# Nine subtractions on GpSimd, each made to wait for a point in VectorE's expert search

## The chip, the cores and the metric

The kernel runs on one core of one Trainium2 chip. The time is that of the whole execution on the device in microseconds (us), as the median of several runs. Five engines take part: TensorE (PE in the profile, its weight loads PEld), VectorE (DVE), ScalarE (ACT), GpSimd (POOL) and SyncE (SP), which issues most of the transfers. Each engine works through its own list of instructions in the order in which they were written, and waits for another engine at a semaphore.

## The reference, cut to what matters

Two layers over a batch of 4 sequences of 512 tokens, 256 wide. The part that the change concerns:

```
xn = layernorm(x)
# layer 0, attention: elu features, running sum of k*v over the sequence
kv_sum = cumsum(phi_k * v, axis=1); context = phi_q * kv_sum * SCALE; attn = context @ Wo.T + bo
# layer 0, ffn: 512 "genes" per token, the best 32 are kept
logits = (rms(xn) * norm_w) @ Wc.T / temperature
top_vals, top_idx = top_k(logits, 32)
expressed = sum(softmax(top_vals) * genes[top_idx])
ffn = tanh(expressed @ Wd.T) * xn * (expressed @ Wu.T) * scale
x = x + attn + ffn
# layer 1: a second attention with a dense swiglu (w_swiglu, w_out), and 16 experts of which
# each token takes 2, with a dense shared expert (shared_gate_up, shared_down)
```

The dense weights of layer 1 (shared_gate_up, shared_down, w_swiglu, w_out) are used as a sum of two parts of lower precision: the rounded weight h, and the low part l = w - h. The nine subtractions of the change make l.

## The kernel before, in words

A batch b is one sequence of 512 tokens. Work on batch b is held in tiles f0a to f0g (even b) and f1a to f1g (odd b), shown in the profile as fa to fg. Every engine has one list, written out by hand over all batches; a name such as `topb(0, 1)` is a call in that list, and its two numbers are the batch and the 128-token tile in it. Nothing reorders these lists.

What is done at the front (the first 110 us), with the lines of the profile:

- The expert search on VectorE, for each batch and tile: `topa` (a MAX8, L887, and a MATCH_REPLACE8, L891, both reading TensorE's result), `topb` (three more pairs on tile tk, L898 and L900), `topc` (one SCALAR_TENSOR_TENSOR with two operands in tk, L907). Each of `topb`'s six instructions raises the semaphore `tb` by one.
- `kvsum` on VectorE (L869): the running sum of a tile fb into ff. `qplus` (L873) and `context` (L878) follow from it.
- On TensorE `emturn` (transposes, L297) of what `topc` made, then `express` (the gene product), `ffn` (L313) and `oproj` (L320, L324). On ScalarE `emcopy` and `expert` between them, `eround` before `elow` (VectorE, L912), and `downt`, the tanh.
- `bolow` on VectorE (L811) makes the low part of the bias that `oproj` adds. `uptimes` (L919) multiplies the two halves of the ffn, and `joined` (L924) adds attention and ffn. `stats2`, the normalization of layer 1 and all the rest of the batch hang on `joined`.
- The preparation of the weights: SyncE loads nine pieces into stage0 to stage8 in the first microseconds, `prep(n)` on ScalarE rounds piece n into h and raises `ph` (L544), and `prep(n)` on GpSimd subtracts h from the staged piece (L1199) and raises `pl`. Pieces 0 and 1 are sgu (1024 and 384 columns), piece 2 is sdn (768), 3 to 6 are wsg, 7 and 8 wout (1024 each).
- On GpSimd the nine `prep` stand at the head of the list. Behind them come `upnorm(0)` (two instructions on fb, L1203 and L1205, which wait for the four `uptimes` of batch 0 and raise `u2`), `residual(0)` (L1210), and then the rest. `joined(0, 0)` waits for `u2`.

The first readers of the low parts are dense products of TensorE at about 110 us (`pl` at 2), and SyncE's `xback(0)`, which waits for `pl` at 9.

The lists around the change:

```
gpsimd: wduround(); prep(0); ... prep(8); upnorm(0); residual(0); qfold(0); ...
vector: ... topb(0, 0); kplus(0); topc(0, 0); topa(0, 1); vtimes(0, 0)
        topa(0, 2); ratio1(1); vtimes(0, 1); topb(0, 1); kvsum(0, 0); topc(0, 1); kvsum(0, 1); topb(0, 2); topa(0, 3); topc(0, 2); topb(0, 3)
        topa(1, 0); topc(0, 3); qplus(0); rscale(0); context(0); wdulow(); elow(0); topa(1, 1); kplus(1); uptimes(0, 0); bolow(); uptimes(0, 1)
        topb(1, 0); uptimes(0, 2); uptimes(0, 3); topb(1, 1); topa(1, 2); joined(0, 0); topc(1, 0); joined(0, 1); stats2(0); ...
```

Of the kernel before, what the change touches and what calls it, by code (L numbers as in the profile page):

```python
# [82 lines left out]
def build(nc, x, vec, cst, wqkv0, wo0, wc, genes, wdu, wqkv1, wsg, wout, gate, sgu, sdn, gu, dn, part_d, out):  # L83
    with ExitStack() as ctx:
        base = nc.sbuf_base + (-nc.sbuf_base) % 32
        ctx.enter_context(nc.sbuf_tensor("arena", [P, 53180], F32))
        s = {n: ctx.enter_context(nc.semaphore("s_" + n)) for n in SIGNALS}
# [117 lines left out]
        def ps(*key):  # L205
# [14 lines left out]
        PREP = [("sgu", sgu_h, sgu_l, sgu, 0, 1024), ("sgu", sgu_h, sgu_l, sgu, 1024, 384), ("sdn", sdn_h, sdn_l, sdn, 0, 768)] + \  # L220
            [("wsg", wsg_h, wsg_l, wsg, o, 1024) for o in range(0, 4096, 1024)] + \
            [("wout", wout_h, wout_l, wout, o, 1024) for o in range(0, 2048, 1024)]
        PREPARED = {"sgu": 2, "sdn": 3, "wsg": 7, "wout": 9}

        GA = [also(f"ga{n}", 1024 * n, 1024) for n in range(2 * NB)]
# [2 lines left out]
        def low_made(b, k):  # L228

            return s["rlp" if SPLIT[b] else "rl"], CHUNKS * sum(z == SPLIT[b] for z in SPLIT[:b]) + k + 1  # L230
# [20 lines left out]
        def tensor(e):  # L251
# [7 lines left out]
            def take(key, n, sem, value):  # L259
                bank_of[key] = n  # L260
                return banks.take(q, n, sem, value)
# [113 lines left out]
            def hidden(b, k, n, first, sem, back, value, key):  # L375
                name, _, _, _, m, r = chunk_of(k)
                wh, wl = pairs[name]
                h, l, made = (XH, HXr, s["xl"]) if k < 3 else (YH, HYr, s["yl"])
                q.wait_ge(s["pl"], PREPARED[name])
                o = take((key, b, k), n, back, value)  # L380
# [14 lines left out]
            def ddown(b, k, n0, n1):  # L395
# [5 lines left out]
                c = CHUNKS * b + k  # L401
                q.wait_ge(s["pl"], PREPARED[name])
                q.wait_ge(*low_made(b, k))
# [785 lines left out]
        def gpsimd(e):  # L1189
            q = Queue(e)  # L1190
# [5 lines left out]
            def prep(n):  # L1196
                _, h, l, _, o, k = PREP[n]
                q.wait_ge(s["ph"], n + 1)
                e.tensor_tensor(l[:, o:o + k], stage[n][:, 0:k], h[:, o:o + k].bitcast(F32), ALU.subtract).then_inc(s["pl"], 1)  # L1199

            def upnorm(b):
# [50 lines left out]
            def yput(j):  # L1252
                q.wait_ge(s["rt"], 31)
                if j:
# [4 lines left out]
                                     in_=m_y[j % 3][:, :], in_offset=None).then_inc(d_my, 16)  # L1259

            wduround(); prep(0); prep(1); prep(2); prep(3); prep(4); prep(5); prep(6); prep(7); prep(8); upnorm(0); residual(0); qfold(0); xlow(0, 0)
            xlow(0, 1); kfold(0); upnorm(1); dlow(0, 0); correct(0); quotient(0); qfold(1); dlow(0, 1); residual(1); kfold(1); ylow(0, 0); ylow(0, 1)
            dlow(0, 2); dlow(0, 3); dlow(0, 4); quotient(1); correct(1); dlow(0, 5); xlow(1, 0); dlow(0, 6); xlow(1, 1); dlow(0, 7); dlow(0, 8)
# [188 lines left out]
```

## Time and profile before

| | |
|---|---|
| median of 3 runs | 569.43 us (568.58 to 572.26) |
| the profiled execution, its own time | 574.54 us |
| its span, first to last instruction | 572.7 us |
| TensorE busy | 515.8 us, 90% |
| VectorE busy | 383.6 us, 67% |
| ScalarE busy | 272.1 us, 48% |
| GpSimd busy | 225.6 us, 39% |

The profiled execution is 5.11 us longer than the median of the unprofiled runs, and 1.84 us of its time lie outside its span. Times in the rows count from the start of the span. A share of busy time is a mean over the whole kernel: what the change can touch lies in the first 80 us.

### The profile page before, as it was taken

Reading aid. Unit: us, or ns where it says so; the run is one execution under the profiler, and the core shown is the slowest. Engines: PE = TensorE matmul, PEld = TensorE weight load, DVE = VectorE, ACT = ScalarE, POOL = GpSimd, SP = SyncE. Lnnn points to the kernel's source line nnn. Section 1 sums busy time; section 2 is a strip of 40 time slices with the busy share of each in tenths; the row PEclk is TensorE's granted clock in tenths of the full one; section 3 lists DMA queues with packets and bytes.
Section 4 is the critical chain, followed back from the end, with each engine's and each line's share of the span. In section 5 each row is a group of like instructions: output and inputs, shape, how many; then the busy total and the mean of one; then the engine's idle time right before and its main releaser. Section 6 shows DMA issues by size and latency. Waiting matters only on the chain.

```text
span 572.7 us, 7158 instructions
## 1 busy us (share of the span) xinstructions
PE 515.8 (90%) x2368; PEld 371.3 (65%) x2368; DVE 383.6 (67%) x784; ACT 272.1 (48%) x527; POOL 225.6 (39%) x174
## 2 busy tenths in 40 slices
PE   3967867999999999999999869899998999899993
PEld 1444534665667876677686448686776777677782
DVE  4899899687799999986678999633332243233246
ACT  3564537766765655388685443233233243233220
POOL 0441332426462113414543530325666566545210
PEclk9979689899999999999999889999999999999998
DMA  8700003003601010000165845502222242222148
GB/s 304 294 0 1 1 0 112 0 1 140 226 2 74 0 38 0 1 0 2 40 222 176 265 162 184 165 28 75 73 102 84 82 137 80 81 64 65 46 159 300
DMA packets 19620, 54.25 MB, mean 95 GB/s; under 512 B 3296, under 2 KB 5728, under 8 KB 19584
## 3 DMA queue, kind: packets, MB, share of 16 engines
q1 hardware_dynamic: 15072, 41.46, 21.3%
q0 software_dynamic: 4512, 12.33, 7.1%
q8 instruction: 20, 0.33, 0.2%
q14 instruction: 16, 0.13, 0.1%
HBM read 36.08 MB, written 17.70 MB: 94 GB/s over the span
## 4 chain that ended last, share of the span: by engine, by line
PE 60%; DVE 25%; issue 6%; DMA 5%; ACT 3%; POOL 1%; another core or an unknown queue 0%; DVEq 0%; SPq 0%; POOLq 0%; ACTq 0%
PE bank L256 41%; PE bank L408 8%; DVE tk L900 3%; DVE m L898 3%; PE bank L324 3%; DVE tk L907 2%; DMA xg<-xn_rows,tab 2%; PE bank L461 2%; DVE ff L869 2%; PE bank L434 1%; DVE tk L891 1%; DMA y_rows<-m_y,dest 1%; DVE m L887 1%; DMA ga<-y_rows 1%; DVE hs L1016 1%
## 5 line engine op out<-in xcount | busy, mean ns | idle before, releaser
L256 PE MATMUL bank<-fe,w_qkv 128*128 128x512 f32 x192 | 91.5, 614 | 2.9 <-DVE ff L934 2.2
L1258 POOL DMA_INDIRECT y_rows<-m_y,dest x47 | 47.7, 1014 | 64.7 <-DMA y_rows<-m_y,dest 33.4
L1128 DVE TENSOR_TENSOR m_h<-m_h,bank 128x176 f32<-128x176 f32 x47 | 15.8, 337 | 83.0 <-ACT m_h L731 67.5
L256 PE MATMUL bank<-mw,m_xt 128*128 x188 | 66.9, 479 | 1.1 <-issue 0.9
L1249 POOL DMA_INDIRECT xg<-xn_rows,tab x47 | 46.8, 996 | 42.9 <-DVE rowv L1122 21.5
L256 PEld LDWEIGHTS bank<-fe,w_qkv 128*128 128x128 f32 x192 | 36.3, 197 | 40.4 <-issue 35.9
L256 PE MATMUL bank<-yhr,wsg_h 128*128 128x512 f32 x128 | 58.9, 460 | 0.0
L256 PE MATMUL bank<-yhr,wsg_l 128*128 128x512 f32 x128 | 50.5, 394 | 0.0
L256 PE MATMUL bank<-hyr,wsg_h 128*128 128x512 f32 x128 | 50.2, 392 | 0.0
L256 PE MATMUL bank<-mw,m_ht 88*128 x188 | 48.4, 379 | 0.3 <-issue 0.3
L256 PEld LDWEIGHTS bank<-mw,m_ht 88*128 88x128 f32 x188 | 35.3, 189 | 11.9 <-issue 1.3
L256 PEld LDWEIGHTS bank<-mw,m_xt 128*128 128x128 f32 x188 | 32.5, 192 | 15.2 <-issue 3.6
L1016 DVE SCALAR_TENSOR_TENSOR hs<-hs,bank 128x512 f32<-128x512 f32 (+1 forms) x44 | 30.1, 683 | 18.3 <-PE bank L256 14.8
L731 ACT ACTIVATE m_h<-bank 128x176 f32<-128x176 f32 x47 | 14.9, 317 | 55.2 <-PE bank L256 47.4
L1135 DVE TENSOR_SCALAR m_y<-bank,gslot 128x256 f32<-128x256 f32 x47 | 22.7, 482 | 25.5 <-PE bank L256 18.6
L256 PE MATMUL bank<-w_wc,fe 128*128 128x512 f32 x64 | 34.1, 662 | 1.5 <-ACT fe L577 0.8
L898 DVE MAX8 m<-tk 128x8 f32<-128x512 f32 x48 | 33.2, 691 | 1.2
L900 DVE MATCH_REPLACE8 tk<-m,tk 128x512 f32<-128x512 f32 x48 | 32.4, 675 | 0.0
L737 ACT ACTIVATE m_ht<-bank 88x256 f32<-88x256 f32 x47 | 17.6, 376 | 30.7 <-PE bank L461 25.7
L532 ACT ACT_TABLE_LOAD x23 | 29.5, 1283 | 5.1 <-PE bank L408 3.2
L1006 DVE SCALAR_TENSOR_TENSOR hs<-hs,bank 128x512 f32<-128x512 f32 (+1 forms) x33 | 22.5, 681 | 14.1 <-ACT hs L713 13.9
L713 ACT ACTIVATE hs<-bank 128x512 f32<-128x512 f32 (+1 forms) x33 | 19.5, 594 | 20.3 <-PE bank L408 12.2
(213 smaller groups left out, 1254.1 us busy)
## 6 DMA issues: line engine op xcount, KB each, us to landing
mw<-in_gu SPq DMA_DIRECT2D x16, 352.0 KB
ga<-y_rows SPq DMA_DIRECT2D x8, 512.0 KB, 7.4
mw<-in_dn SPq DMA_DIRECT2D x16, 176.0 KB
fa<-in_x SPq DMA_DIRECT2D x4, 512.0 KB, 3.5
stage<-in_wsg SPq DMA_DIRECT2D x4, 512.0 KB, 12.5
spilled_x<-fa SPq DMA_DIRECT2D x4, 512.0 KB, 5.4
spilled_r<-fb SPq DMA_DIRECT2D x4, 512.0 KB, 5.8
hx<-spilled_x SPq DMA_DIRECT2D x4, 512.0 KB, 4.8
```

The lines of the kernel that those rows point to most:

```text
L256: mm = e.matmul(o, a, b, start=n == 0, stop=n == len(terms) - 1)
L408: mm = e.matmul(o, a, w[0:m, r, :], start=k == 0 and i % 2 == 0 and z == 0, stop=False, skip_group_check=True)
L532: e.preload_act_table_set(name)
L713: e.activation(HS[c % 2][0:m, 0, :], ps("dg", b, k)[0:m, :], ACT.Tanh, scale=0.5).then_inc(s["tg"], 1)
L737: e.activation(m_ht[j % 2][:, :], ps("jt", j)[0:88, 0:D], ACT.Copy).then_inc(s["jtc"], 1)
L898: e.max(m[:, 8 * k:8 * k + 8], w).then_inc(t, 1)
L900: e.match_replace(w, m[:, 8 * k:8 * k + 8], w, LOWEST).then_inc(t, 1)
L1006: e.scalar_tensor_tensor(h, h, 1.0, ps("dg", b, k)[0:m, :], ALU.add, ALU.mult).then_inc(s["g2"], 1)
L1016: e.scalar_tensor_tensor(h[0:m, 1, :], h[0:m, 0, :], 1.0 if DIRECT[b] else 0.5, ps("du", b, k)[0:m, :], ALU.mult, ALU.mult).then_inc(s["dh ...
L1135: e.tensor_scalar(m_y[j % 3][:, :], ps("jd", j)[:, 0:D], gslot[:, j:j + 1], None, ALU.mult).then_inc(s["jy"], 1)
L1249: e.indirect_dma_start(out=xg[j % 3][:, :], out_offset=None, in_=xn_d, in_offset=bass.IndirectOffsetOnAxis(ap=tab[:, j:j + 1], axis=0)).th ...
L1258: e.indirect_dma_start(out=y_d, out_offset=bass.IndirectOffsetOnAxis(ap=dest[:, j:j + 1], axis=0), in_=m_y[j % 3][:, :], in_offset=None).t ...
```

## The change

```diff
+        MEANWHILE = (1, 1, 2, 2, 3, 3, 4, 4, 5)
...
             def prep(n):
                 _, h, l, _, o, k = PREP[n]
                 q.wait_ge(s["ph"], n + 1)
+
+                q.wait_ge(s["tb"], 6 * MEANWHILE[n] + 1)
                 e.tensor_tensor(l[:, o:o + k], stage[n][:, 0:k], h[:, o:o + k].bitcast(F32), ALU.subtract).then_inc(s["pl"], 1)
```

`tb` at 6 m + 1 is the end of the first MAX8 of the search numbered m, where m counts tiles over batches: 1, 2, 3 are `topb(0, 1)`, `topb(0, 2)`, `topb(0, 3)`, and 4, 5 are `topb(1, 0)`, `topb(1, 1)`. So `prep(0)` and `prep(1)` start in `topb(0, 1)`, `prep(2)` and `prep(3)` in `topb(0, 2)`, `prep(4)` and `prep(5)` in `topb(0, 3)`, `prep(6)` and `prep(7)` in `topb(1, 0)`, and `prep(8)` in `topb(1, 1)`. No instruction is added, removed or moved on any engine; only the waits of five GpSimd instructions differ (the second of each pair has its point already met).

GpSimd's list before, from the first subtraction on (sgu_l is the low part, s_ph the semaphore that ScalarE's rounding raises):

```order
L1199 TENSOR_TENSOR sgu_l_151<-stage0_137,sgu_h_150 128x1024 [waits s_ph]
L1199 TENSOR_TENSOR sgu_l_151<-stage1_138,sgu_h_150 128x384 [waits s_ph]
L1199 TENSOR_TENSOR sdn_l_153<-stage2_139,sdn_h_152 128x768 [waits s_ph]
L1199 TENSOR_TENSOR wsg_l_147<-stage3_140,wsg_h_146 128x1024 [waits s_ph]
L1199 TENSOR_TENSOR wsg_l_147<-stage4_141,wsg_h_146 128x1024 [waits s_ph]
```

The same list with the change, to the end of `upnorm(0)` (fb0_59 is the tile that `joined(0, 0)` waits for):

```order
L1203 TENSOR_TENSOR sgu_l_151<-stage0_137,sgu_h_150 128x1024 [waits s_tb,s_ph]
L1203 TENSOR_TENSOR sgu_l_151<-stage1_138,sgu_h_150 128x384 [waits s_ph]
L1203 TENSOR_TENSOR sdn_l_153<-stage2_139,sdn_h_152 128x768 [waits s_tb,s_ph]
L1203 TENSOR_TENSOR wsg_l_147<-stage3_140,wsg_h_146 128x1024 [waits s_ph]
L1203 TENSOR_TENSOR wsg_l_147<-stage4_141,wsg_h_146 128x1024 [waits s_tb,s_ph]
L1203 TENSOR_TENSOR wsg_l_147<-stage5_142,wsg_h_146 128x1024 [waits s_ph]
L1203 TENSOR_TENSOR wsg_l_147<-stage6_143,wsg_h_146 128x1024 [waits s_tb,s_ph]
L1203 TENSOR_TENSOR wout_l_149<-stage7_144,wout_h_148 128x1024 [waits s_ph]
L1203 TENSOR_TENSOR wout_l_149<-stage8_145,wout_h_148 128x1024 [waits s_tb,s_ph]
L1207 TENSOR_TENSOR fb0_59<-fb0_59,fd0_63 128x1024 [waits s_up]
L1209 TENSOR_TENSOR fb0_59<-fb0_59,fa0_57 128x1024 [waits s_u2]
```

The order is as it was; five of the nine rows have gained s_tb. The last of them stands directly ahead of `upnorm(0)`.

## Rows read from the trace of the kernel before

**Rows 1.** The page: busy time, and TensorE and the DMA engines in 40 slices.

```profile
PE 515.8 (90%) x2368; PEld 371.3 (65%) x2368; DVE 383.6 (67%) x784; ACT 272.1 (48%) x527; POOL 225.6 (39%) x174
...
PE   3967867999999999999999869899998999899993
...
DMA  8700003003601010000165845502222242222148
```

**Rows 2.** The chain of waits, 0 to 130 us: start, us, what.

```profile
22.71 2.85 DVE tk L907 x2
...
34.85 3.05 DVE ff L869
37.89 2.77 DVE tk L907 x2
40.66 1.14 DVE ff L869
...
47.61 2.23 DVE tk L907 x2
...
55.67 0.62 DVE tk L907 x2
...
58.13 2.04 PE bank L256 x8
...
64.59 2.44 DVE bo_r L811
```

**Rows 3.** GpSimd in order of time: start, us, engine, line, operation [idle before <-releaser].

```profile
22.56 3.84 POOL L1199 TENSOR_TENSOR sgu_l<-stage,sgu_h 128x1024 fp32r<-128x1024 f32 x2 [6.09 <-ACT sgu_h L544]
...
31.75 2.37 POOL L1199 TENSOR_TENSOR wsg_l<-stage,wsg_h 128x1024 fp32r<-128x1024 f32 x1 [3.57 <-ACT wsg_h L544]
34.46 2.35 POOL L1199 TENSOR_TENSOR wsg_l<-stage,wsg_h 128x1024 fp32r<-128x1024 f32 x1 [0.35 <-ACT wsg_h L544]
37.76 2.35 POOL L1199 TENSOR_TENSOR wsg_l<-stage,wsg_h 128x1024 fp32r<-128x1024 f32 x1 [0.95 <-ACT wsg_h L544]
46.93 2.35 POOL L1199 TENSOR_TENSOR wsg_l<-stage,wsg_h 128x1024 fp32r<-128x1024 f32 x1 [6.82 <-ACT wsg_h L544]
64.40 4.84 POOL L1199 TENSOR_TENSOR wout_l<-stage,wout_h 128x1024 fp32r<-128x1024 f32 x2 [15.12 <-ACT wout_h L544]
73.18 2.36 POOL L1203 TENSOR_TENSOR fb<-fb,fd 128x1024 f32<-128x1024 f32 x1 [3.94 <-DVE fb L919]
```

**Rows 4.** VectorE in order of time, with the same columns.

```profile
32.66 0.68 DVE L900 MATCH_REPLACE8 tk<-m,tk 128x512 f32<-128x512 f32 x1
...
72.62 0.48 DVE L919 SCALAR_TENSOR_TENSOR fb<-bank,sm,fb 128x256 f32<-128x256 f32 x1 [0.27 <-ACT fb L644]
...
78.84 0.68 DVE L924 TENSOR_TENSOR fb<-bank,fb 128x512 f32<-128x512 f32 x1
```

**Rows 5.** TensorE in order of time, with the same columns.

```profile
35.90 1.91 PE L256 MATMUL bank<-tk,w_genes 128*96 128x128 f32 x8
...
43.15 1.98 PE L256 MATMUL bank<-w_wc,fe 128*128 128x512 f32 x4 [0.68 <-ACT fc L606]
...
49.89 0.66 PE L297 MATMUL bank<-w_cst,tk 128*128 128x128 f32 x4 [0.45 <-DVE tk L907]
...
56.33 1.12 PE L297 MATMUL bank<-w_cst,tk 128*128 128x128 f32 x4 [3.19 <-DVE tk L907]
...
61.65 1.62 PE L313 MATMUL bank<-wdu_r,fg0r 96*128 96x512 f32 x3 [1.50 <-DVE fg0r L912]
...
67.07 0.49 PE L320 MATMUL bank<-bo_r,w_one 64*128 64x512 f32 x1 [0.39 <-DVE bo_r L811]
...
80.28 1.08 PE L297 MATMUL bank<-w_cst,tk 128*128 128x128 f32 x4 [4.17 <-DVE tk L907]
```

**Rows 6.** Windows: stretch, us, busy time of PE, PEld, DVE, ACT, POOL, granted TensorE clock, DMA share, GB/s.

```profile
56.00:66.00 10.00, 7.49 (x19) 4.55 (x19) 8.57 (x14) 6.87 (x12) 1.60 (x1) 0.52 0.00 1
...
102.00:104.00 2.00, 2.00 (x11) 2.00 (x10) 2.00 (x3) 0.53 (x1) 0.00 (x0) 0.50 0.00 0
```

## The prediction

> **What bounds the kernel now.** I read the page first. TensorE is busy for 515.8 of 572.7 us, and its slices say where it is not: full from the ninth slice on (114 us), at 3 to 9 tenths before [rows 1]. Whatever shortens the front therefore lets the full part start earlier; nothing else in this change can help. The chain of waits then says who sets the front: between 22 and 57 us it runs almost without a break over VectorE. In it five pieces stand out [rows 2]: `topc` at 22.71 with 2.85 us, `kvsum` at 34.85 with 3.05, `topc` at 37.89 with 2.77 and at 47.61 with 2.23, and `bolow` at 64.59 with 2.44. The same operations elsewhere in that chain take 0.62 (`topc` at 55.67) and 1.14 (`kvsum` at 40.66).
>
> Beside each long piece lies a subtraction of GpSimd [rows 3]. The row at 34.46 ends at 34.46 + 2.35 = 36.81, and `kvsum` ends 1.09 later, at 37.90. The row at 37.76 ends at 40.11, `topc` 0.55 later. The row at 46.93 ends at 49.28, `topc` 0.56 later. The first of the pair at 64.40 ends near 66.75, `bolow` 0.28 later. The first of the pair at 22.56 ends near 24.95, `topc` 0.61 later. So VectorE's instruction stands still until the subtraction is over, and then runs at its normal length. Each of the five has both operands in on-chip memory outside TensorE's result banks. The search does not behave so: the subtraction at 31.75 to 34.12 lies over a MATCH_REPLACE8 at 32.66 that takes 0.68 us [rows 3, 4], its normal length. The change moves the nine subtractions under searches.
>
> **What goes away.** Freed lengths, from [rows 2] with 0.62 for `topc`, 1.14 for `kvsum` and 0.48 for `bolow` (from the nearest row of that size, `uptimes` [rows 4]): 2.23 + 1.91 + 2.15 + 1.61 = 7.90 us up to `topc(0, 2)`, and 1.96 in `bolow`; 9.86 us together.
>
> **Do the new places hold?** A search takes 4.4 us (`topb(0, 3)` with the `topa` behind it: from the end of `topc` at 49.84 to 55.67 is 5.83, of which `topa` is 1.4). After the first MAX8 (0.7 us) 3.7 us of the search are left, and 1.4 of `topa` where one follows. A 1024-column subtraction is 2.35, and by columns 768 are 1.8 and 384 are 0.9. `prep(0)` and `prep(1)`: 3.25 against 3.7, then `kvsum`. `prep(2)` and `prep(3)`: 4.15 against 5.1. `prep(4)` and `prep(5)`: 4.7 against 5.1, then `topc(0, 3)`. `prep(6)` and `prep(7)`: 4.7, behind them only `uptimes`, which reads one operand from a bank. The margins are 0.45, 0.95 and 0.4 us; a miss costs only the overrun. I count these collisions at nothing, and at 0 to 1 us in the range.
>
> **What of the 7.90 us arrives.** The first 2.23 us reach everything: `ratio1(1)`, ScalarE's normalization of batch 1, and TensorE's `express(0, 0)`, which goes from 35.90 to 33.67 [rows 5]. From there TensorE works in a row until 56.33 - 3.19 = 53.14, with only two gaps, 0.68 and 0.45, whose releasers (`kvsum(0, 1)` by way of ScalarE, and `topc(0, 2)`) come 6.3 and 7.9 us earlier. So its work of 17.24 - 1.13 = 16.11 us ends at 49.78, and `emturn(0, 3)` follows at once, where before it waited 3.19 us for `topc(0, 3)` (now done by 48.4). It starts at 49.78 for 56.33: 6.55 us earlier. TensorE has become the limit here, and 1.35 of the 7.90 us stay in its queue.
>
> The clock gives something back. Over 56 to 66 us the granted clock was 0.52 [rows 6], the 1.2 GHz level, after 3.19 us in which TensorE stood still. That idle stretch is closed. With 2.4 GHz the transposes at 56.33 take half of 1.12 and the `express(0, 3)` at 58.13 half of 2.04 [rows 2, 5]: 1.6 us more. `elow(0)` and `ffn(0, 0)` come 6.55 + 1.6 = 8.15 us earlier, at 53.5 for 61.65. VectorE has by then finished `topc(0, 3)`, `qplus` and `context` (about 51.4) and isn't the later one.
>
> Next, from `ffn(0, 0)` at 61.65 to the end of `logits(1, 2)` at 67.07 - 0.39 = 66.68 are 5.03 us, at the low level [rows 5, 6]. Unchanged they end at 58.5; at the high level throughout they take 2.5 and end at 56.0, and then `bolow` is the later one: 64.59 - 8.15 + 0.48 = 56.9. So `oproj(0, 0)` starts between 56.9 and 58.5, for 67.07: a gain of 8.55 to 10.15. Idle stretches of 0.7 and 1.5 us remain between 50.3 and 53.5. The nearest row to that is after 100 us, where the clock had gone to 0.50 though TensorE had been idle only in two short pieces [rows 6], so I take the clock to fall once more, but for less long: 9.4 us. The `ffn(0, 3)` behind `oproj` and the `uptimes(0, 3)` at 72.62 [rows 4] follow at 63.2. VectorE is there at 62.1, GpSimd has ended `prep(7)` by 62.7.
>
> **What the last wait costs.** `prep(8)` must now wait for the first MAX8 of `topb(1, 1)`, which stands directly behind `uptimes(0, 3)`, and `upnorm(0)` is queued behind it. Before, GpSimd began `upnorm(0)` at 73.18, right behind `uptimes(0, 3)`, was done at about 77.97 (two instructions of 2.36 and 2.35, of which the first stands in [rows 3]), and `joined(0, 0)` came at 78.93 when VectorE reached it, so GpSimd's part was hidden by 0.9 us. Now, counted on the old clock: `uptimes` ends at 73.02, the MAX8 at 73.71, GpSimd starts 0.08 later, `prep(8)` takes 2.35, `upnorm` 4.8: 80.98. `joined(0, 0)` is late by 80.98 - 78.93 = 2.05 us. All of it is on the chain, since `topc(1, 0)`, for which TensorE waited 4.17 us at 80.28 [rows 5], is queued behind `joined(0, 0)`.
>
> **The sum.** 9.4 - 2.05 = 7.35 us. Behind `joined(0, 0)` every list hangs on the same chain and moves as one: the collision of `residual(0)` with the second `kvsum` of batch 1 keeps its place, the first reader of a low part comes at 110 us, and no load ties the work to the start (the DMA engines are idle from the third slice on [rows 1]). The span goes from 572.7 to 565.3, the profiled execution from 574.54 to 567.2, and the median, 5.1 below the profiled one, from 569.4 to 562.1.
>
> **The rivals.**
>
> Less arrives. The clock stays low all the way (8.55), two of the close margins are missed (1 us together) and the handovers to GpSimd are slower than 0.08 us: 8.55 - 2.05 - 1 to 2 = 4.5 to 5.5 us, or 564.5. For it: the margins are 0.4 us, and every number rests on one execution. 17%.
>
> More arrives. The stretch of TensorE from 33.7 to 39 us, slow before, comes back to the high level earlier, and the one at 53 too: 10.15 + up to 1.4 - 2.05 = 8.1 to 9.5 us, or 560.6. 13%.
>
> The gain is given back in the full part, where TensorE would wait as much for something that did not move. I see nothing of that kind in [rows 1]; 569.4. 7%.
>
> The wait takes the place of the stall. If what holds `topc` and `kvsum` were not the subtraction, only the last wait's 2.05 us would be left: 571.5. The five endings speak against it. 4%.
>
> Slower: the search is held up too. A MATCH_REPLACE8 reads its eight values and its tile, both in on-chip memory. If it were blocked like `topc`, the 19.2 us of subtraction (seven times 2.35, 1.8 and 0.9) would lie on VectorE's path, in place of the 9.86 they take now: 9.3 us more, and the 2.05, less the 3 or so that TensorE's queue absorbs: near 578. It decides from the point where a MATCH_REPLACE8 under a subtraction takes more than its 0.68 us. The row at 32.66 speaks against it [rows 4], though it is the only MATCH_REPLACE8 of a `topb` that lay wholly under a subtraction. 7%.
>
> The Trainium skill, page "SBUF — State Buffer", section "Who interferes with whom", says that a VectorE instruction with two inputs in this memory contends with a GpSimd instruction that reads it, and that whichever started first keeps the port while the other blocks fully. [...]
>
> **How the numbers follow.** The forecast (a gain of 6 to 8 us) has 52%. The range leaves out the last three rivals, 18%, and takes in the others' ends: 559.5 to 566.5 us. About 1% (5.7 us) is what a measurement of this kernel can tell from no change: below 563.7 lie the forecast, the rival with more, and a quarter of the one with less, 69%; within 1% the rest of that one, the one given back and the one with only the wait, 24%; slower 7%.
>
> **What would show it.** In the changed profile `topc` and `kvsum` of batch 0 should take about 0.7 and 1.2 us and `bolow` 0.5; the subtractions should start behind the first MAX8 of their searches, and MAX8 and MATCH_REPLACE8 keep 0.69 and 0.68; `emturn(0, 3)` should start near 50 without a wait; VectorE should show a wait of about 1 to 3 us for GpSimd ahead of `joined(0, 0)`, near 71.5 us; and the first dense product of TensorE, at 109.7 before, should come at about 102.3. The prediction is wrong if the clock stays low where I count it high, if GpSimd's pairs overrun their searches, or if the 7 us at the front are not there at the end.

## The result, and the profile after

The changed kernel took 562.27 us (median of 5 runs, 560.3 to 565.25), the kernel before 569.43 us. The ratio is 0.9886, 95% interval 0.985 to 0.9922: faster by 1.1%, or 7.16 us between the medians. 562.1 had been forecast. The profiled execution took 564.64 us, with a span of 562.8, for 574.54 and 572.7 before.

The page of the changed kernel, busy time and the two rows of slices that answer to [rows 1]:

```profile
PE 509.6 (91%) x2368; PEld 369.7 (66%) x2368; DVE 373.3 (66%) x784; ACT 272.4 (48%) x527; POOL 225.5 (40%) x174
...
PE   3978678999999999999999769899999999999993
...
DMA  8800003006401100000255846402232242222148
```

VectorE's busy time has fallen by 10.3 us with the same 784 instructions, GpSimd's by 0.1. The time in which an instruction stands still is counted as busy (9.87 us of the 10.3 are the five instructions below), so the saving is visible there. TensorE's slices are full from the eighth on in both pages; a slice is now 14.07 us long for 14.32, so that this begins near 98.5 us instead of 100.2 (the prediction put it a slice too late, at 114, which enters no term).

VectorE in order of time in the changed kernel (start, us, engine, line, operation, idle before it and its releaser), the places of [rows 2, 4]. Line numbers are 2 higher than before:

```profile
22.70 0.69 DVE L909 SCALAR_TENSOR_TENSOR tk<-tk 128x512 f32<-128x512 f32 x1
...
32.60 1.22 DVE L871 TENSOR_TENSOR_SCAN ff<-fb 128x512 f32<-128x512 f32 x1
33.73 0.67 DVE L909 SCALAR_TENSOR_TENSOR tk<-tk 128x512 f32<-128x512 f32 x1
...
41.26 0.68 DVE L909 SCALAR_TENSOR_TENSOR tk<-tk 128x512 f32<-128x512 f32 x1
...
56.74 0.41 DVE L813 TENSOR_TENSOR bo_r<-w_wdu,bo_r 32x256 fp32r<-32x256 f32 x1
...
62.75 0.48 DVE L921 SCALAR_TENSOR_TENSOR fb<-bank,sm,fb 128x256 f32<-128x256 f32 x1 [0.27 <-ACT fb L646]
...
71.10 0.69 DVE L926 TENSOR_TENSOR fb<-bank,fb 128x512 f32<-128x512 f32 x1 [2.03 <-POOL fb L1209]
```

All five long instructions have their normal lengths. The last row is the price: `joined(0, 0)` waits 2.03 us for GpSimd. GpSimd in order of time shows why, and answers to [rows 3]:

```profile
29.02 3.32 POOL L1203 TENSOR_TENSOR sgu_l<-stage,sgu_h 128x1024 fp32r<-128x1024 f32 x2 [11.85 <-DVE m L900]
36.27 1.81 POOL L1203 TENSOR_TENSOR sdn_l<-stage,sdn_h 128x768 fp32r<-128x768 f32 x1 [3.93 <-DVE m L900]
38.04 2.36 POOL L1203 TENSOR_TENSOR wsg_l<-stage,wsg_h 128x1024 fp32r<-128x1024 f32 x1
42.70 4.67 POOL L1203 TENSOR_TENSOR wsg_l<-stage,wsg_h 128x1024 fp32r<-128x1024 f32 x2 [2.30 <-DVE m L900]
...
63.98 2.36 POOL L1203 TENSOR_TENSOR wout_l<-stage,wout_h 128x1024 fp32r<-128x1024 f32 x1 [0.88 <-DVE m L900]
66.29 2.35 POOL L1207 TENSOR_TENSOR fb<-fb,fd 128x1024 f32<-128x1024 f32 x1
68.72 2.34 POOL L1209 TENSOR_TENSOR fb<-fb,fa 128x1024 f32<-128x1024 f32 x1
```

The groups end at 32.3, 40.4 and 47.4 us, ahead of `kvsum` at 32.60, `topc` at 41.26 and `topc(0, 3)` at 47.82. `prep(8)` at 63.98 then pushes `upnorm(0)` from behind `uptimes(0, 3)` (63.2) to 66.29.

TensorE, the places of [rows 5]:

```profile
33.74 1.91 PE L258 MATMUL bank<-tk,w_genes 128*96 128x128 f32 x8
...
49.91 0.60 PE L299 MATMUL bank<-w_cst,tk 128*128 128x128 f32 x4
...
53.81 0.93 PE L315 MATMUL bank<-wdu_r,fg0r 96*128 96x512 f32 x3 [1.50 <-DVE fg0r L914]
54.58 1.88 PE L258 MATMUL bank<-w_wc,fe 128*128 128x512 f32 x4
57.21 0.50 PE L322 MATMUL bank<-bo_r,w_one 64*128 64x512 f32 x1 [0.76 <-DVE bo_r L813]
...
102.00 0.47 PE L258 MATMUL bank<-xhr,sgu_h 128*128 128x512 f32 x1 [0.52 <-issue]
```

`emturn(0, 3)` follows at 49.91 without a wait; before it waited 3.19 us. The last row is the first dense product, which I use below as a mark. The same product in the kernel before:

```profile
109.68 0.47 PE L256 MATMUL bank<-xhr,sgu_h 128*128 128x512 f32 x1 [0.51 <-issue]
```

So in these two profiles 7.68 us have arrived where TensorE becomes full.

### The profile page after: what moved, and what is told of

The parts are those of the page before. It is cut to its first block, busy times and chain, and to the rows that moved or that the text cites. A ratio compares the mean times of both kernels' runs of the same rounds, so it can differ in the third digit from the quotient of the medians.

```text
span 562.8 us, 7163 instructions
## 1 busy us (share of the span) xinstructions
PE 509.6 (91%) x2368; PEld 369.7 (66%) x2368; DVE 373.3 (66%) x784; ACT 272.4 (48%) x527; POOL 225.5 (40%) x174
## 3 DMA queue, kind: packets, MB, share of 16 engines
q1 hardware_dynamic: 15072, 41.46, 21.5%
## 4 chain that ended last, share of the span: by engine, by line
PE 66%; DVE 19%; DMA 4%; ACT 4%; issue 4%; POOL 2%; another core or an unknown queue 0%; SPq 0%; DVEq 0%; POOLq 0%; ACTq 0%
PE bank L258 46%; PE bank L410 9%; PE bank L326 3%; PE bank L463 2%; DVE m L900 2%; DVE tk L902 2%; PE bank L436 2%; DMA xg<-xn_rows,tab 1%; DMA ga<-y_rows 1%; DVE ff L871 1%; DMA w_vec<-in_vec 1%; DVE hs L1008 1%; DVE hs L1018 1%; DVE tk L909 1%; DVE tk L893 1%
## 5 line engine op out<-in xcount | busy, mean ns | idle before, releaser
L258 PEld LDWEIGHTS bank<-fe,w_qkv 128*128 128x128 f32 x192 | 36.6, 198 | 40.4 <-issue 36.2
L258 PE MATMUL bank<-mw,m_ht 88*128 x188 | 48.5, 379 | 0.5 <-ACT m_ht L739 0.5
L258 PE MATMUL bank<-w_wc,fe 128*128 128x512 f32 x64 | 31.8, 623 | 0.8 <-ACT fe L579 0.8
```

Of the source, the lines that this page charges most:

```text
L258: mm = e.matmul(o, a, b, start=n == 0, stop=n == len(terms) - 1)
```

## The experiments

Executions differ in how long the first loads take: the first `topc` began at 21.5 to 24.0 us in the profiles. So stretches are given between marks of one execution: A, from the first `topc` to `uptimes(0, 3)`; B, from there to `joined(0, 0)`; C, from there to the first dense product. "Held" says whether the second `kvsum` of batch 1 stood still under `residual(0)` (3.37 us) or ran (1.22).

| kernel | A | B | C | held | median us | ratio to before | interval |
|---|---|---|---|---|---|---|---|
| before | 49.91 | 6.22 | 30.84 | yes | 569.43 | 1 | |
| the change | 40.05 | 8.35 | 30.90 | yes | 562.27 | 0.9886 | 0.985 to 0.9922 |
| e8, the change again | 39.62 | 8.34 | 28.48 | no | 563.88 | 0.9854 | 0.9815 to 0.9893 |
| e4, last wait alone | 49.91 | 8.34 | 28.26 | no | 574.12 | 1.0042 | 1.001 to 1.0073 |
| e3, upnorm first | 38.79 | 6.23 | 29.28 | yes | 561.44 | 0.9819 | 0.9769 to 0.9869 |
| e2, first six waits | 44.07 | 6.22 | 29.29 | yes | 562.98 | 0.9872 | 0.9821 to 0.9924 |
| e5, three in one search | 41.69 | 6.23 | 30.90 | yes | 562.6 | 0.9816 | 0.9768 to 0.9863 |
| e6, residual too | 38.79 | 6.22 | 27.96 | no | 559.3 | 0.9784 | 0.9741 to 0.9826 |
| e1, bolow only | 48.20 | 6.23 | 30.90 | yes | 572.62 | 1.0031 | 0.9998 to 1.0064 |
| e10, the same again | 49.37 | 6.22 | 30.90 | yes | 571.77 | 1.001 | 0.998 to 1.004 |
| e9, before again | 49.91 | 6.22 | 29.29 | yes | 569.88 | 0.9978 | 0.9954 to 1.0002 |
| e7, GpSimd writes only | 40.23 | 6.23 | 28.74 | no | 561.35 | 0.9805 | 0.9763 to 0.9848 |
| e11, upnorm first again | 40.96 | 6.22 | 28.48 | no | 561.09 | 0.9854 | 0.9811 to 0.9897 |
| e12, residual too again | 40.26 | 6.23 | 28.74 | no | 559.53 | 0.9818 | 0.978 to 0.9856 |

The kernel before had a median of 570.37 us where e1, e2, e3 and e4 were measured, 572.17 for e5 to e8, 570.9 for e9 and e10, and 568.55 for e11 and e12. A ratio is always to the kernel before that was measured beside it, so ratios compare better than medians.

B is the same to 0.01 us in every execution with the same order, but A and C are not. TensorE's clock moves them. In A the change and its repeat differ by 0.43, e3 and e11 by 2.17. In C two groups stand among the executions in which `kvsum` was held: 29.28 or 29.29 in e2, e3 and e9, and 30.84 or 30.90 in the others. In the latter the sixteen products of batch 1's `express` took 3.1 to 3.5 us instead of 1.96 (the granted clock over 92 to 96 us was 0.64 in the change, over 88 to 92 us 1.00 in e3).

### e4: the last wait alone

```diff
-        MEANWHILE = (1, 1, 2, 2, 3, 3, 4, 4, 5)
+        MEANWHILE = (0, 0, 0, 0, 0, 0, 0, 0, 5)
...
-                q.wait_ge(s["tb"], 6 * MEANWHILE[n] + 1)
+                if MEANWHILE[n]:
+                    q.wait_ge(s["tb"], 6 * MEANWHILE[n] + 1)
```

> Only prep(8) waits, for topb(1, 1), the other eight run as before. Theory: all five long instructions of VectorE stay, and joined(0, 0) is late by 2.05 us: it starts at 80.9 for 78.84, first dense product at 111.7, time 571.5. Rival (the wait is hidden behind the search and topa): first dense product at 109.7, time 569.4.

It took 574.12 us, ratio 1.0042 (1.001 to 1.0073), which is 2.4 us of 570. A stayed at 49.91 and B rose from 6.22 to 8.34, as the theory has it. The first dense product was expected at 111.7 and came at 110.51, with the first `topc` at 24.00: in this execution `kvsum` was not held, and C was 2.58 us shorter than before. VectorE in order of time in this kernel:

```profile
24.00 2.85 DVE L909 SCALAR_TENSOR_TENSOR tk<-tk 128x512 f32<-128x512 f32 x1
...
82.25 0.69 DVE L926 TENSOR_TENSOR fb<-bank,fb 128x512 f32<-128x512 f32 x1 [2.04 <-POOL fb L1210]
```

The stall is there and the wait comes on top of it. The price of the last wait is 2.12 us in B, shown by itself.

### e3 and e11: upnorm(0) ahead of prep(8)

```diff
-        MEANWHILE = (1, 1, 2, 2, 3, 3, 4, 4, 5)
+        MEANWHILE = (1, 1, 2, 2, 3, 3, 4, 4, 6)
...
-            ... prep(7); prep(8); upnorm(0); residual(0); ...
+            ... prep(7); upnorm(0); prep(8); residual(0); ...
```

> Theory (the last wait costs 2.05 us because upnorm(0) is queued behind prep(8)): with upnorm(0) ahead of prep(8), and prep(8) under the search topb(1, 2), joined(0, 0) starts at about 69.1 us instead of 71.1, VectorE doesn't wait for GpSimd ahead of it, and the first dense product comes at about 100.0 us (102.0 with the change, 109.7 before). Time about 560.2. Rival (joined(0, 0) is held by something else, or the front's gain is already all there is): the first dense product stays at 102.0, time 562.3.

> upnorm(0) ahead of prep(8) once more, beside the version with residual(0) waiting too. Counted from the start of the first topc, joined(0, 0) at 45.0 us as in the first run. Ratio 0.982.

561.44 us, ratio 0.9819 (0.9769 to 0.9869), and again 561.09, 0.9854 (0.9811 to 0.9897). B is back at 6.23, to the hundredth the value of the kernel before, and VectorE doesn't wait:

```profile
65.26 0.69 DVE L889 MAX8 m<-bank 128x8 f32<-128x512 f32 x1
65.98 0.09 DVE L893 MATCH_VALUE_LOAD tk<-m,bank 128x8 f32 x1
66.06 0.68 DVE L893 MATCH_REPLACE8 tk<-m,bank 128x512 f32<-128x512 f32 x1
66.66 0.68 DVE L926 TENSOR_TENSOR fb<-bank,fb 128x512 f32<-128x512 f32 x1
```

That the queue behind `prep(8)` costs 2.12 us is shown from both sides. In the whole time the intervals of this version and of the change overlap. In e3 `joined(0, 0)` came 38.79 + 6.23 = 45.02 us behind the first `topc`, where 69.1 - 22.7 = 46.4 had been expected, and the first dense product at 95.94 for 100.0. What came beyond the expectation is an earlier first `topc` (1.06 us) and an A and a C that are 1.26 and 1.62 shorter than in the change, in an execution in which TensorE ran faster; the wait accounts only for the 2.12. For e11 45.0 was expected from e3, and 69.19 - 22.01 = 47.18 came: there `logits(1, 2)` took 3.62 us for 1.88 in e3.

### e2: the first six waits alone

```diff
-        MEANWHILE = (1, 1, 2, 2, 3, 3, 4, 4, 5)
+        MEANWHILE = (1, 1, 2, 2, 3, 3, 0, 0, 0)
```

> prep(0) to prep(5) wait as in the change, prep(6) to prep(8) have no wait on the search. Theory: prep(6) runs right behind prep(5), from 47.4 to 49.7, and holds topc(0, 3) to 50.4; prep(7) holds bolow to about 59.3; both cost about 2.1 us at oproj, and upnorm(0) starts on time, which gives 2.05 back. joined(0, 0) at about 71.2, first dense product at 102.1, time 562.4. Rival (each wait of the change carries its share): the first dense product at 104 or later, time 564.5.

562.98 us, ratio 0.9872 (0.9821 to 0.9924), for 562.4 forecast. The interval also takes in the rival's 564.5, so only the profile can tell them apart. `prep(6)` held `topc(0, 3)` and `prep(7)` held `bolow`, as expected:

```profile
48.06 2.53 DVE L909 SCALAR_TENSOR_TENSOR tk<-tk 128x512 f32<-128x512 f32 x1
...
57.68 2.14 DVE L813 TENSOR_TENSOR bo_r<-w_wdu,bo_r 32x256 fp32r<-32x256 f32 x1
```

`joined(0, 0)` came 50.29 us behind the first `topc`, for 48.40 with the change and 71.2 - 22.7 = 48.5 expected. TensorE shows why: it waited 2.48 us for `bolow`, and then the first eight products of `oproj` took twice the time of the next eight.

```profile
60.30 3.68 PE L326 MATMUL bank<-w_wo,ff 128*128 128x256 f32 x8
...
64.34 1.99 PE L326 MATMUL bank<-w_wo,ff 128*128 128x256 f32 x8
```

The slow eight cost 1.69 us; over 60 to 64 us the granted clock was 0.57, and 1.00 over the 3 us behind. The first dense product came at 102.63 for 102.1 expected and 104 by the rival, with the first `topc` 0.35 later than in the change. So in these profiles the last three waits of the change buy 4.02 us in A, 1.69 of them by the clock, and the last of them costs 2.13 in B; in the whole time the two versions can't be told apart.

### e1 and e10: only bolow freed

```diff
-        MEANWHILE = (1, 1, 2, 2, 3, 3, 4, 4, 5)
+        MEANWHILE = (0, 0, 0, 0, 0, 0, 0, 4, 4)
```

> Only prep(7) and prep(8) wait (for topb(1, 0)), the other seven run as before. Theory (what VectorE is freed of arrives only as far as TensorE was waiting): bolow goes from 2.43 to 0.41 us, but oproj had waited only 0.39 us for it, so the first dense product moves from 109.7 to 109.3, time 569.0. Rival (freed lengths add up on the path): 107.7, time 567.5.

> Once more the kernel in which only prep(7) and prep(8) wait, beside the kernel before against itself on the same chip. If the two waits cost something by themselves: ratio 1.003 again. If the first measurement was scatter: 0.998 to 1.000, as the theory (0.4 us gained at oproj) has it.

572.62 us, ratio 1.0031 (0.9998 to 1.0064), and again 571.77, 1.001 (0.998 to 1.004). `bolow` took 0.41 us in both, and the time shows no gain. That the 1.96 us freed there do not arrive by themselves is borne out: the rival's 567.5 would be a ratio of 0.997, below both intervals; whether 0.4 us arrive can't be told from these intervals. In the profile of e10 `oproj` came 66.41 - 22.59 = 43.82 us behind the first `topc`, for 67.07 - 22.71 = 44.36 before: 0.54 us. In that of e1 it was 42.65: there `express(0, 3)` took 1.25 us for 2.02, at a granted clock of 0.83 over 56 to 58 us, and the level of 0.50 came behind it.

### e9: the kernel before against itself

> The kernel before against itself. It shows what of the rows varies from one execution to the next: the start of the first topc, the clock level over logits(1, 2), and whether residual(0) or the second kvsum of batch 1 comes first. Five long instructions as before; joined(0, 0) 56.1 us behind the first topc if the clock falls as before, 54.4 if it falls as in the run with prep(7) and prep(8) waiting. Ratio 1.000.

569.88 us, ratio 0.9978 (0.9954 to 1.0002). The same five instructions took 2.85, 3.12, 2.84, 2.30 and 2.44 us, and `joined(0, 0)` came 56.13 us behind the first `topc`, as before. So these lengths were no accident of the one execution that the prediction rests on. C was 29.29 us, though, for 30.84, with `kvsum` held in both. The offset of 0.2% is a measure of what e1 and e10 can tell.

### e5: three subtractions in one search

```diff
-        MEANWHILE = (1, 1, 2, 2, 3, 3, 4, 4, 5)
+        MEANWHILE = (1, 1, 2, 2, 2, 3, 3, 4, 4)
```

> The written order of the change, its table (1, 1, 2, 2, 2, 3, 3, 4, 4): three subtractions under topb(0, 2), and none behind uptimes(0, 3). Theory: the third of them holds topc(0, 2) by 1.5 us, which is just what VectorE had to spare against TensorE's queue at 49.9; upnorm(0) starts on time. First dense product at 100.0 to 100.3, time 560.4. Rival (a stall of VectorE always costs its length): first dense product at 101.5, time 561.8.

562.6 us, ratio 0.9816 (0.9768 to 0.9863), for 560.4 expected and 561.8 by the rival. B was 6.23, but A was 41.69, 1.64 above that of the change. `topc(0, 2)` was held to 2.01 us, and TensorE did wait for it:

```profile
40.31 2.01 DVE L909 SCALAR_TENSOR_TENSOR tk<-tk 128x512 f32<-128x512 f32 x1
```

```profile
32.35 1.04 PE L258 MATMUL bank<-tk,w_genes 128*96 128x128 f32 x8
33.22 3.68 PE L258 MATMUL bank<-fe,w_qkv 128*128 128x512 f32 x8
...
48.82 0.65 PE L299 MATMUL bank<-w_cst,tk 128*128 128x128 f32 x4 [2.42 <-DVE tk L909]
...
54.50 3.44 PE L258 MATMUL bank<-w_wc,fe 128*128 128x512 f32 x4
```

The theory failed here. What VectorE has to spare against TensorE's queue was there only while TensorE ran slowly: in the changed kernel's profile `express(0, 0)` and the eight products behind it took 1.91 and 5.14 us, here 1.04 and 3.68. With the faster start TensorE is early, waits 2.42 us for VectorE, and then meets `logits(1, 2)` at the low clock (3.44 for 1.88). The first dense product came 78.82 us behind the first `topc`, where the theory's 100.3 would be 77.6 and the rival's 101.5 would be 78.8. The rival was right in the profile; in the whole time the version can't be told from the change.

### e7: GpSimd writes but doesn't read

```diff
-                e.tensor_tensor(l[:, o:o + k], stage[n][:, 0:k], h[:, o:o + k].bitcast(F32), ALU.subtract).then_inc(s["pl"], 1)
+                e.memset(l[:, o:o + k].bitcast(F32), 0.0).then_inc(s["pl"], 1)
```

The edit is to the kernel before, without any wait on the search.

> The kernel before, with GpSimd's nine subtractions replaced by memsets of the same tiles to 0 (the low parts of the dense weights are left out of the computation). Theory (VectorE is held by GpSimd's reading of its operands in the shared memory): no stall though the memsets stand where the subtractions stood: topc 0.69, kvsum 1.22, bolow 0.41, and no last wait, so the first dense product at about 100.0, time 560.2. Rival (any GpSimd instruction on this memory holds VectorE's two-operand instructions, by its own length): stalls as long as the memsets, first dense product between 100 and 109.7.

561.35 us, ratio 0.9805 (0.9763 to 0.9848). GpSimd in order of time, and then VectorE:

```profile
22.01 1.30 POOL L1199 MEMSET sgu_l<- 128x1024 f32 x2 [5.71 <-ACT sgu_h L544]
...
31.75 0.95 POOL L1199 MEMSET wsg_l<- 128x1024 f32 x1 [1.75 <-ACT wsg_h L544]
...
55.90 0.95 POOL L1199 MEMSET wout_l<- 128x1024 f32 x1 [11.91 <-ACT wout_h L544]
```

```profile
22.18 0.68 DVE L907 SCALAR_TENSOR_TENSOR tk<-tk 128x512 f32<-128x512 f32 x1
...
32.08 1.22 DVE L869 TENSOR_TENSOR_SCAN ff<-fb 128x512 f32<-128x512 f32 x1
...
56.40 0.42 DVE L811 TENSOR_TENSOR bo_r<-w_wdu,bo_r 32x256 fp32r<-32x256 f32 x1
```

The memsets lie over a `topc` and `bolow` for their whole length and over the first 0.62 us of a `kvsum`, and none is held. A memset on this memory is thus not enough for the stall, and it needs what the subtraction has beyond it, its two reads (whether one read would do was not tried). The first dense product came at 97.38 for the 100.0 expected, and the interval takes in the 560.2 us. The Trainium skill, page "SBUF — State Buffer", section "Who interferes with whom", says this: two inputs on VectorE contend with a GpSimd instruction that reads, not with one that only writes. The runs agree.

### e6 and e12: residual(0) waits as well

To the version of e3:

```diff
             def residual(b):
+                if b == 0:
+                    q.wait_ge(s["tb"], 6 * 7 + 1)
```

> The order with upnorm(0) ahead of prep(8), and residual(0) made to wait for the first MAX8 of topb(1, 3). Theory (the same stall once more: the second kvsum of batch 1 takes 3.37 us under residual(0)): that kvsum takes 1.22, residual(0) fits under the search, and the first dense product comes at about 97.9 us. Time about 558.1. Rival (residual(0) a few us later delays its spill, the load of hx behind it in SyncE's queue and the first dense product): first dense product at 100 or later, time 560 or more.

> With residual(0) waiting too. joined(0, 0) at 45.0 us behind the first topc, the second kvsum of batch 1 at 1.22 in every execution. If that collision costs 2 us in most executions of the other: ratio 0.978. If it happens only in some: 0.980.

559.3 us, ratio 0.9784 (0.9741 to 0.9826), and again 559.53, 0.9818 (0.978 to 0.9856). This version has the lowest medians. Beside the change on the same chip (e8) it is 4.6 us faster, beside e3's version (e11) 1.6; the first difference is clear of the scatter, the second is not, since the intervals of e11 and e12 overlap. For e12 45.0 us from the first `topc` to `joined(0, 0)` were expected and 46.49 came, with TensorE slow behind the first `express` as in the change. Of the ratios 0.978 and 0.980 the measured intervals exclude neither. The second `kvsum` of batch 1 ran free in both, with C at 27.96 and 28.74 us. GpSimd in e6:

```profile
83.35 2.36 POOL L1216 TENSOR_TENSOR fb<-fb,fg 128x1024 f32<-128x1024 f32 x1 [6.37 <-DVE m L900]
```

The rival, a late spill, did not show: the first dense product came at 96.11.

### e8: the change again

> The changed kernel once more, for the comparison on one chip: first dense product at 102.0 us, time 562.3, ratio 0.988.

563.88 us, ratio 0.9854 (0.9815 to 0.9893). The first dense product was expected at 102.0 and came at 99.19, with the first `topc` at 22.75 for 22.70. Here `kvsum` started ahead of `residual(0)` and GpSimd was the one that waited. VectorE, then GpSimd, in e8:

```profile
82.50 1.22 DVE L871 TENSOR_TENSOR_SCAN ff<-fb 128x512 f32<-128x512 f32 x1
```

```profile
82.89 2.98 POOL L1214 TENSOR_TENSOR fb<-fb,fg 128x1024 f32<-128x1024 f32 x1 [12.22 <-ACT fg L590]
```

In the changed kernel's first profile the two were the other way round by 0.16 us: GpSimd at 82.73, `kvsum` at 82.89 with 3.37 us. C was 30.90 there and 28.48 here, but only a part of the 2.42 us is the collision: e3, held and without the slow stretch of TensorE in C, had 29.28, 0.80 more than here. Which of the two starts first differed between two executions of the change and between two of e3's version; of the twelve profiles (all but e6 and e12) in which nothing keeps them apart, `kvsum` was held in eight.

## Why the prediction was right, point by point

**Whose stall it was.** Right. The five instructions went to 0.69, 1.22, 0.67, 0.68 and 0.41 us as soon as no subtraction lay over them. e4 keeps the stall with the first eight waits gone, and e7 removes it with GpSimd's reads gone.

**The new places.** Right. The groups of subtractions kept inside their searches, with 0.3, 0.9 and 0.4 us to spare for the 0.45, 0.95 and 0.4 worked out. In the changed kernel's front all 15 MATCH_REPLACE8 of `topb` took 0.674 to 0.678 us, so the slower rival was wrong. The prediction had MATCH_REPLACE8 read its eight values and its tile, two inputs at once. The trace of the changed kernel shows the values loaded by an instruction of its own, a MATCH_VALUE_LOAD of 0.09 us ahead of each MATCH_REPLACE8:

```profile
31.93 0.09 DVE L902 MATCH_VALUE_LOAD tk<-m,tk 128x8 f32 x1
32.00 0.68 DVE L902 MATCH_REPLACE8 tk<-m,tk 128x512 f32<-128x512 f32 x1
```

If only the tile is left to be read, this is an instruction with one input. The section of the Trainium skill that the prediction names, page "SBUF — State Buffer", section "Who interferes with whom", speaks of instructions with two inputs and does not say that MATCH_REPLACE8 is one, so the measured 0.68 us do not contradict it. The profile names both tiles in the MATCH_REPLACE8 row, though, and no run tests by itself which of them it reads.

**What arrives of 7.90 us.** `emturn(0, 3)` was forecast at 49.78 and came at 49.91 without a wait. The two numbers agree partly by luck: the products behind `express(0, 0)` were slower than taken (4.98 us from start to next start, for 4.26 before), and the gaps closed as said. That TensorE becomes the limit and keeps 1.35 us in its queue holds in the change's first profile and in e12. In e3, e6 and e11 TensorE ran the stretch faster, came early and waited 1.09 us for `topc(0, 3)`, so that VectorE was the limit, as in the rival in which more arrives. In e8 `emturn(0, 3)` came without a wait 25.84 us behind the first `topc`, for 27.21 in the first profile.

**What the clock gives back.** The term was 9.4 us at `oproj`, from a span of 8.55 to 10.15. It measured 67.07 - 57.21 = 9.86. The clock did not fall in the changed kernel's profile: over 53 to 57 us the granted clock was 1.00, `logits(1, 2)` took 1.88 us and `bolow` was the later one, by 0.76. In e8 it did fall: over the same stretch the granted clock was 0.59, and the same four products took 3.17 us. Counted from the first `topc`, `oproj` came 9.85 us earlier than before in the change, 10.29 in e8, 11.11 in e3, 11.12 in e6, 9.56 in e11 and 9.66 in e12. So the mechanism was right, and 9.4 was a little too small, since all six lie above it: in the change and e12 the clock did not fall, in e8 and e11 it fell but the products behind `express(0, 0)` ran faster than before (3.77 and 3.68 us for 4.43), of which the 9.4 has no share, and in e3 and e6 both helped.

**The last wait.** 2.05 forecast, 2.03 read as a wait, 2.12 as the difference in B. Shown alone in e4 and taken away in e3. The forecast has two small slips: [rows 4] has `joined(0, 0)` at 78.84 and not at 78.93, and its terms 73.71 + 0.08 + 2.35 + 4.8 add up to 80.94 and not to 80.98. Put right they give 2.10.

**The sum.** 9.4 - 2.05 = 7.35 was forecast, 7.68 measured at the first dense product, 7.16 between the medians. That 562.27 came for 562.1 is closer than such a forecast can be: the interval of the ratio is 4 us wide, and the repeat (e8) gained 8.3 us between the medians. The span of the profiled execution fell by 9.9 us instead. The rest of it came late: the last product of the routed experts was handed on at 536.27 for 546.28, 10.0 us earlier, though the first of them had come 7.6 earlier (374.2 for 381.8). The repeats don't show it: from the first of these products to the last took 163.9 us in e9, the kernel before again, and 164.7 in e8, the change again, for 164.5 and 162.1 in the two profiles compared. So it is scatter of these executions, not a gain of the change. TensorE's waits for gathered rows account for little of it (3.0 us in four waits before, 2.2 in two after).

**"Behind `joined(0, 0)` every list moves as one."** True for the two profiles compared (C of 30.84 and 30.90), with two reservations that I had not seen. The collision of `residual(0)` with `kvsum` does not keep its place, since the two start 0.16 to 0.40 us apart in the kernels with subtractions, and the order changes from one execution to the next. And TensorE's clock in C differs between executions, which moves the first dense product by 1.6 us. The reason given for the loads was also misread: in [rows 1] the DMA engines are not idle from the third slice on, but at 3 tenths in the seventh slice and at 3 and 6 in the tenth and eleventh. No term rests on it.

## What to carry to other kernels

When an instruction takes several times its usual length, look for one on the neighbouring engine that ends a fixed time before it does; if there is one, try to move it under work that doesn't collide. A wait that is added for this holds the whole queue behind it: put the work that others wait for ahead of it (here 2.12 us, of 9.86 won in A in the same profile), and look for further pairs of the same kind, since one was left. Freed time counts only as far as the next engine was waiting for it, and what is to spare there depends on TensorE's clock in that execution, so a placement that just fits by one profile needs a second one.

## What the runs showed of the hardware

- GpSimd's subtraction (two reads, one write) holds VectorE's instructions with two operands in the shared on-chip memory until it is over (a `topc` took 2.85 us for 0.69), while GpSimd's memset of the same tile does not (0.68, 1.22 and 0.42 us beneath three of them). The MAX8 and MATCH_REPLACE8 of the front kept 0.66 to 0.70 us beneath subtractions; a separate MATCH_VALUE_LOAD of 0.09 us stands ahead of each MATCH_REPLACE8.
- Who starts first holds the other: `kvsum` took 3.37 us when `residual(0)` began 0.16 us ahead of it, and 1.22 when it began 0.39 us ahead of `residual(0)`, which then took 2.98.
- The same four products of `logits(1, 2)` took 1.88 us in six of the profiled executions and 3.17 to 3.62 in eight, with the same order of TensorE's instructions around them. Whether the clock falls there differs between executions of one kernel (1.88 in the change's first profile, 3.17 in its second; 1.88 in e3 and 3.62 in e11).
